# A two-axis Toeplitz block: v stored as pairs of channels, column sums on four 64x64 tiles

## The reference

```python
xn = srms(x)
u = silu(xn @ u_w.T + u_b)
v = silu(xn @ v_w.T + v_b)
out = tno(v, axis=-3, rpe2) + tno(v, axis=-2, rpe1)   # per channel: sum over j of a[i - j] * v[j]
out = (u * out) @ o_w.T + o_b + x
```

## Time and profile before

| | us |
|---|---|
| median of 3 runs (840.05 to 843.59) | 843.44 |
| the profiled execution | 840.65 |
| its span | 838.6 |
| PE busy | 780.2 |
| ScalarE busy | 637.2 |
| VectorE busy | 527.5 |
| GpSimd busy | 282.0 |

### The profile page before, as it was taken

How to read it: one execution, slowest core, us unless ns; L and a number is a source line. 1 busy time by engine, 2 the same in 40 slices (tenths; PEclk the granted TensorE clock), 3 DMA queues, 4 the chain that set the end, 5 groups by cost and what they waited for, 6 DMA issues and landing times.

```text
span 838.6 us, 16989 instructions
## 1 busy us (share of the span) xinstructions
PE 780.2 (93%) x5996; PEld 725.7 (87%) x5996; DVE 527.5 (63%) x917; ACT 637.2 (76%) x794; POOL 282.0 (34%) x191
## 2 busy tenths in 40 slices
PE   0999979999999999899999999989999999897886
PEld 0999879999999999799999999979999999765654
DVE  7666534259999999444554445455655665676666
ACT  0666657789999998777788787769999999665554
POOL 4334332221112112645555454210000001866664
PEclk9999999999999999999999999989999999999999
DMA  9455463497777675688888888685445444777876
GB/s 222 135 158 176 148 164 142 166 222 159 169 167 173 140 162 158 195 279 260 273 268 275 273 262 275 196 199 121 113 120 125 113 116 143 223 250 247 253 249 190
DMA packets 128985, 160.97 MB, mean 192 GB/s; under 512 B 67288, under 2 KB 94108, under 8 KB 128924
## 3 DMA queue, kind: packets, MB, share of 16 engines
q1 hardware_dynamic: 128924, 160.15, 68.2%
HBM read 109.49 MB, written 50.63 MB: 191 GB/s over the span
## 4 chain that ended last, share of the span: by engine, by line
PE 80%; DMA 12%; DVE 2%; ACT 1%; issue 1%; SPq 1%; POOL 1%; POOLq 0%; ACTq 0%; DVEq 0%
PE ps L946 24%; PE ps L1011 16%; PE ps L1024 15%; DMA out<-x_e 9%; PE ps L993 8%; PE ps L966 6%; PE ps L956 5%; PE ps L937 3%; POOL u_in L471 1%; PE ps L969 1%; SPq L269 1%; DMA u_dram<-u_in 1%; DMA stage<-a_dram 1%; DMA u_in<-u_dram 1%; PE ps L920 1%
## 5 line engine op out<-in xcount | busy, mean ns | idle before, releaser
L471 POOL TENSOR_TENSOR u_in<-u_in,v 128x1152 f32<-128x1152 f32 (+2 forms) x66 | 171.4, 2602 | 191.7 <-DMA u_in<-u_dram 175.8
L564 ACT COPY vc<-v 128x1024 f32<-128x1024 f32 x72 | 170.8, 2372 | 6.3 <-DMA out<-x_e 6.3
L848 DVE TENSOR_TENSOR g<-ps,g 128x512 fp32r<-128x512 f32 (+1 forms) x192 | 125.6, 681 | 73.0 <-ACT g L536 45.7
L1011 PE MATMUL ps<-vc,toepA 128*128 128x128 f32 x1152 | 144.1, 279 | 6.1 <-DVE toepA L802 4.2
L1011 PEld LDWEIGHTS ps<-vc,toepA 128*128 128x128 f32 x1152 | 137.3, 195 | 6.7 <-issue 6.4
L1024 PE MATMUL ps<-toepB,vt 128*128 128x128 f32 x1152 | 140.5, 275 | 0.0
L1024 PEld LDWEIGHTS ps<-toepB,vt 128*128 128x128 f32 x1152 | 134.8, 192 | 0.0
L802 DVE COPY toepA<-stage 64x512 f32<-64x512 f32 x144 | 110.0, 764 | 33.5 <-DMA stage<-a_dram 15.2
L742 DVE TENSOR_TENSOR xl<-ps,xh 96x512 fp32r<-96x512 f32 x64 | 44.0, 687 | 130.4 <-ACT xh L512 130.4
L946 PE MATMUL ps<-wu,xh 97*128 97x288 f32 x512 | 122.8, 305 | 2.4
L946 PE MATMUL ps<-wv,xh 97*128 97x288 f32 x512 | 119.3, 308 | 4.6 <-ACT u_in L517 4.2
(11 more groups left out here) (75 smaller groups left out, 1004.9 us busy)
## 6 DMA issues: line engine op xcount, KB each, us to landing
stage<-a_dram SPq DMA_DIRECT2D x144, 256.0 KB, 4.2
u_in<-u_dram SPq DMA_DIRECT2D x64, 576.0 KB, 5.3
u_dram<-u_out SPq DMA_DIRECT2D x48, 576.0 KB, 3.3
x_e<-in_x_eT SPq DMA_DIRECT2D x64, 192.0 KB, 3.8
out<-x_e SPq DMA_DIRECT2D x64, 192.0 KB, 3.8
u_dram<-u_in SPq DMA_DIRECT2D x16, 576.0 KB, 2.9
x_all<-in_x SPq DMA_DIRECT2D x16, 384.0 KB, 5.3
x_n<-in_x SPq DMA_DIRECT2D x16, 384.0 KB, 5.4
```

The source lines that it names most:

```text
L471: return nc.gpsimd.tensor_tensor(out=tile, in0=tile, in1=v[:, bass.ds(t * NB, NB), start:end], op=ALU.mult)
L564: nc.scalar.copy(vc[n % 2][:], v[:, :, UNIT * n:UNIT * n + UNIT].rearrange("p m c -> p c m")).then_inc(vc_ready, 1)
L848: nc.vector.tensor_tensor(out=low, in0=ps[0:w, bank], in1=high.bitcast(f32), op=ALU.subtract).then_inc(gl_ready, 1)
L1011: last = nc.tensor.matmul(ps[:, SET_BANK[n % 2] + c // NB, (c % NB) * P:(c % NB + 1) * P], toepA[n % 2][:, c], vc[n % 2][:, c], start=(c % ...
```

## The change

v is stored as pairs of channels: `v[128, 144 pairs, 128 columns, 2]`, so that one channel of all columns has a step of 8 bytes. The copy `vc` and its semaphore go; PE reads v itself.

`along_columns` now works on four tiles of 64x64. `toepA` is `[128, 8, 64]`, without zero blocks and made by one copy. For each c of 0 to 3, channel c goes through the tiles (rows 0 to 63, outputs 0 to 63) and (64 to 127, 64 to 127), channel 4 + c through the two crossed ones, so that its two rows of pixels land in PSUM exchanged. For those channels the transposes use `swap`, the identity with its halves exchanged, and `evacuate_y` puts them back with two copies of 64 partitions, three copies in all. Each tile's last matmul increments `columns_done`.

The SiLU into v and the gate follow the new order of v. GpSimd no longer zeroes toepA. What lay beside v in the first projections (x, the weights, the network's matrices and activations) now lies in the second halves of v's rows, `free_rows`, which are free until step 16, and has more and smaller pieces in its DMAs; chunks 4 to 7 of x are loaded to three other places, `x_late`, and chunk 7 is loaded at the head of chunk 5, not of chunk 4. Of the diff, what follows leaves out changed offsets, the counts of semaphores and the same rewriting of operands in other lines.

```diff
-        v = place("v", [P, STEPS * NB, D], 0)
-        w_raw = place("w_raw", [KE, 2, D], 0)
-        x_all = place("x_all", [P, STEPS, NB, E], V_BYTES - STEPS * NB * E * 4)
-        R0 = 79104
-        r_lw = place("r_lw", [P, 2, LAYERS, RC, RPE], R0)
...
+        v = place("v", [P, D // 2, STEPS * NB, 2], 0)
+
+
+        free_rows = place("free_rows", [P, D // 2, 2, P], 0)
+
+        def rows(first, count, width=P, partitions=slice(0, P)):
+            return free_rows[partitions, first:first + count, 1, 0:width]
...
+        x_late = [place(f"x_late{k}", [P, CHUNK_ROWS, E], V + offset) for k, offset in enumerate((36864, 13824, 0))]
+
+        def x_chunk(c):
+
+            if c < FREE_CHUNKS:
+                return rows(CHUNK_ROWS * c, CHUNK_ROWS, E)
+            return x_late[(c - FREE_CHUNKS) % 3][:]
...
         stage = [place(f"stage{k}", [P, 2, H, UNIT], V + U_BYTES * k) for k in range(STAGES)]
-        toepA = [place(f"toepA{k}", [P, UNIT, P], V + (50688, 40960)[k]) for k in range(2)]
+        toepA = [place(f"toepA{k}", [P, UNIT, H], V + (50688, 52736)[k]) for k in range(2)]
         toepB = [place(f"toepB{k}", [P, UNIT, P], V + (32768, 28672)[k]) for k in range(2)]
-        vc = [place(f"vc{k}", [P, UNIT, P], V + (13824, 18432)[k]) for k in range(2)]
...
+        Y_PARTS, TILES = 3, 4
+
         def conv_through(engine, half, unit):
 
-            engine.wait_ge(conv_out, UNITS * half + unit + 1)
+            engine.wait_ge(conv_out, Y_PARTS * (UNITS * half + unit + 1))
...
                 for i in range(2):
-                    sp.dma_start(x_all[H * i:H * i + H, CH * c:CH * (c + 1)].rearrange("p s n e -> p (s n) e"),
-                                 rows_of(0, CH * c, CH, i)).then_inc(x_all_loaded, 16)
+                    sp.dma_start(x_chunk(c)[H * i:H * i + H], rows_of(0, CH * c, CH, i)).then_inc(x_all_loaded, 16)
...
+                for o in range(RC):
+                    sp.dma_start(rows(lw_row(n, o, 0, 0), LAYERS * RC),
+                                 lwT[n].rearrange("l (c p) (o q) -> o p (l c) q", p=P, q=P)[o]).then_inc(rpe_loaded, 16)
+                for c in range(RC):
+                    sp.dma_start(rows(OW + NCH * (RC * n + c), NCH, E),
+                                 out_wT[n, P * c:P * c + P].rearrange("p (h q) -> p h q", h=NCH)).then_inc(rpe_loaded, 16)
...
             def phase_a(c, first, last):
-                if c + 3 < CHUNKS:
+                if c + 3 < CHUNKS - 1:
                     load_x_all(c + 3)
+                elif c + 2 == CHUNKS - 1:
+
+                    sp.wait_ge(x_scaled, CH * (c + 2 - 2))
+                    load_x_all(c + 2)
...
             nc.gpsimd.affine_select(out=ident[:], in_=ident[:], compare_op=ALU.not_equal, fill=1.0, base=0,
                                     pattern=[[-1, P]], channel_multiplier=1).then_inc(consts_ready, 1)
 
+            pool.wait_ge(consts_ready, 1)
+            for k in range(2):
+                nc.gpsimd.tensor_copy(swap[:, H * k:H * k + H], ident[:, H - H * k:P - H * k]).then_inc(consts_ready, 1)
...
                     nc.gpsimd.memset(tile[H * k:H * k + H, :, H - H * k:P - H * k], 0.0).then_inc(toep_zeroed, 1)
                     pool.wait_ge(toep_zeroed, count + k + 1)
 
-            pool.wait_ge(a_stored, 32)
-            zero(toepA[0], 0)
-            pool.wait_ge(norms_summed, CHUNKS)
-            pool.wait_ge(x_scaled, STEPS)
-            zero(toepA[1], 2)
             pool.wait_ge(projected, PAIRS * STEPS)
-            zero(toepB[0], 4)
+            zero(toepB[0], 0)
...
             def gate(half, t, r, loads, start=0, end=D):
 
                 pool.wait_ge(u_loaded[r % CH], 16 * CHUNKS * half + 16 * loads)
-                tile = u_in[:, r % CH, :, start:end]
+                tile = u_in[:, r % CH, :, start:end].rearrange("p n (c e) -> p n c e", e=2)
                 return nc.gpsimd.tensor_tensor(
-                    out=tile, in0=tile, in1=v[:, bass.ds(t * NB, NB), start:end], op=ALU.mult)
+                    out=tile, in0=tile, in1=v[:, start // 2:end // 2, bass.ds(t * NB, NB)].rearrange("p c n e -> p n c e"),
+                    op=ALU.mult)
...
-            def silu(xs, pair, target):
+            def silu(xs, pair, target, source):
                 act.wait_ge(projected, PAIRS * xs + (pair + 1))
-                b = 2 * (pair % 2)
-                nc.scalar.activation(target, ps[:, b:b + 2, 0:D], ACT.Silu).then_inc(silu_done, 1)
+                nc.scalar.activation(target, source, ACT.Silu).then_inc(silu_done, 1)
...
+            def projection(pair):
+                return ps[:, 2 * (pair % 2):2 * (pair % 2) + 2, 0:D]
 
             def silu_v(half, t, pair):
                 if half:
                     act.wait_ge(ug_ready, t + 1)
-                silu(STEPS * half + t, pair, v[:, bass.ds(t * NB + 2 * pair, 2)])
+                silu(STEPS * half + t, pair, v[:, :, bass.ds(t * NB + 2 * pair, 2)],
+                     projection(pair).rearrange("p n (c e) -> p c n e", e=2))
...
-            def by_channels(half, n):
...
-                nc.scalar.copy(vc[n % 2][:], v[:, :, UNIT * n:UNIT * n + UNIT].rearrange("p m c -> p c m")
-                     ).then_inc(vc_ready, 1)
...
 
                 def evacuate_y(n):
                     act.wait_ge(conv_done, UNITS * half + n + 1)
-                    bank = SET_BANK[n % 2]
-                    nc.scalar.copy(v[:, :, UNIT * n:UNIT * n + UNIT],
-                                   ps[:, bank:bank + 2].rearrange("p b (c m) -> p m (b c)", m=P)).then_inc(conv_out, 1)
-
-                by_channels(half, 0)
+                    bank, pair, pairs = SET_BANK[n % 2], UNIT // 2 * n, UNIT // 4
+                    nc.scalar.copy(v[:, pair:pair + pairs],
+                                   ps[:, bank].rearrange("p (c e m) -> p c m e", e=2, m=P)).then_inc(conv_out, 1)
+
+                    for i in range(2):
+                        to, of = slice(H * i, H * i + H), slice(H - H * i, P - H * i)
+                        nc.scalar.copy(v[to, pair + pairs:pair + 2 * pairs],
+                                       ps[of, bank + 1].rearrange("p (c e m) -> p c m e", e=2, m=P)
+                                       ).then_inc(conv_out, 1)
+
                 evacuate_vt(0)
                 for n in range(UNITS):
                     if n:
                         evacuate_y(n - 1)
                     if n + 1 < UNITS:
-                        by_channels(half, n + 1)
                         evacuate_vt(n + 1)
...
+                    if axis == 0:
+                        nc.vector.tensor_copy(
+                            toepA[n % 2][:], stage[n % STAGES][:, axis].rearrange("p k c -> p c k")[:, :, ::-1]
+                        ).then_inc(toepA_ready, 1)
+                        return
...
                         nc.vector.tensor_copy(
-                            (toepA, toepB)[axis][n % 2][rows, :, rows],
+                            toepB[n % 2][rows, :, rows],
                             stage[n % STAGES][rows, axis].rearrange("p k c -> p c k")[:, :, ::-1]
-                        ).then_inc((toepA_ready, toepB_ready)[axis], 1)
+                        ).then_inc(toepB_ready, 1)
...
@@ -991,33 +1019,30 @@
                     wait(pe, vt_ready, N)
                     for c in range(UNIT):
                         last = nc.tensor.transpose(ps[:, VT_BANK + c // NB, (c % NB) * P:(c % NB + 1) * P],
-                                                   v[:, :, UNIT * n + c], ident[:])
+                                                   v[:, UNIT // 2 * n + c // 2, :, c % 2], (ident, swap)[c // NB][:])
...
                 def along_columns(n):
+
+                    N = UNITS * half + n
+                    pe.wait_ge(toepA_ready, N + 1)
+                    if n >= 2:
+                        conv_through(pe, half, n - 2)
+                    for c in range(NB):
+                        for i, o, b in ((0, 0, 0), (1, 1, 0), (0, 1, 1), (1, 0, 1)):
+                            of, to, ch = slice(H * i, H * i + H), slice(H * o, H * o + H), NB * b + c
+                            last = nc.tensor.matmul(ps[to, SET_BANK[n % 2] + b, c * P:(c + 1) * P],
+                                                    toepA[n % 2][of, ch], v[of, UNIT // 2 * n + ch // 2, :, ch % 2],
+                                                    start=(c == 0), stop=False, skip_group_check=True)
+                            if c == NB - 1:
+                                last.then_inc(columns_done, 1)
+
+                def along_rows(n):
 
                     N = UNITS * half + n
                     if n < 2:
-                        pe.wait_ge(toep_zeroed, zeroed_for(n)[n][0])
-                    pe.wait_ge(toepA_ready, 2 * (N + 1))
-                    pe.wait_ge(vc_ready, N + 1)
-                    if n >= 2:
-                        conv_through(pe, half, n - 2)
-                    for c in range(UNIT):
```

(19 more changed lines are left out.)

111 lines of the change are left out of this document (52 added, 59 removed).

## The result

| | before | after |
|---|---|---|
| median of the runs | 842.98 us | 814.50 us (813.19 to 815.15, 4 runs) |
| ratio | 1 | 0.967, 95% interval 0.965 to 0.969 |
| span of the profiled execution | 838.6 us | 812.3 us |

The account below looks back on a forecast made before the run. TensorE, busy 93%, was taken to bound the kernel. 840.65 + 28.8 (tile shape) + 1.5 (ScalarE) - 2.4 (VectorE) + 0.3 (loads) + 0.5 (start) = 869.35 us; the median lies 2.8 above, so 872 us, range 800 to 900.

Parts of the forecast that it names:

- What bounds it: Whole kernel: TensorE is busy for 93% of the span, and inside the sums a change pays on PE alone.
- a record costs its 128 columns: Matmul records on PE: 0.112 us for 128 moving columns, whatever part of the array is filled.
- The columns: Column sums on four 64x64 tiles: half the overlap lost to program order, 1.79 us a unit as before, no change.
- Rival 1: Column sums: all four tiles run at once, columns with shape changes 1.29 us, unit 3.97, total 807 us; chance 0.40.
- the forecast: The prediction's main case: half the tile overlap lost to program order, total 872 us; chance 0.42.
- The change of tile shape: Into and out of the column sums: 0.20 us each, 0.40 us a unit, +28.8 us over 72 units.
- The reads of v: Column sums: PE reading one float in two of v as moving operand costs nothing, 0 us.
- ScalarE, silu, gate: Three evacuating copies at 0.59 us each, silu into v at 0.65 us, gate at 2.67 us; new layout costs 0.
- the 4.0 us that was set against it: GpSimd's gate by the skill's rule that reads at steps over 8 bytes are half again as dear: +5 us.
- the +1.5: Ends of the two sums stages: ScalarE's three copies have nothing to hide behind, +0.8 us twice, +1.5 us.
- VectorE and the starts: Starts of both sums stages: no vc copy to await, toepA made in one copy; -1.7 and -0.7, together -2.4 us.
- Loads of x: First projections: store of u earlier, -4 us; chunk 7 loaded later, +4.3 us; net +0.3, bounds -5 and +5.

## Why the prediction was wrong, step by step

**What bounds it, and that a record costs its 128 columns: right**, for tiles too. Each tile keeps 0.112 us (two tiles: 32 records in 1.78 us).

**The columns: wrong, and this is the whole miss.** I took a value between two ends 2.7 us a unit apart, 1.79 us (called the middle, though halfway would be 2.23), by a rule that no row supported: program order without any look-ahead. Measured 0.89 us; the term was 0 and should have been -0.90 x 72 = -65 us. The rule is not empty. It holds from the fifth record in a row on one tile (four matmuls in a row: 2.4 us), but a float32 matmul is two. The Trainium skill does not in fact stand on both sides. The Trainium skill's TensorEngine Tiling (Array Packing), Key Properties, has tiles load and multiply in parallel, and the trace agrees: four records, one for each tile, every 0.11 us. The sentence on strict order in start and end, from the Trainium skill's TensorE: Matmul & The Clock Gate, Part 3, was read out of its place. That part is itself about packing small tiles, and its picture has the matmuls of different tiles start some 4 ns apart and run at once, so it was no ground for 1.79 us. Where the sentence is taken by itself, this case differs: with four in a row a tile's first record starts before the last three of the tile before. Rival 1 named the condition, a queue deep enough for a whole pair, and gave 807 us; with the first projections 5.8 us longer instead of its 0.8 it would be 812, against the 814.5 measured (part of that closeness is chance, since it had nothing for the reads of v and 0.02 to 0.04 us a unit too much for the changes of shape). I gave it 0.40 and the forecast 0.42: the chances were nearly even, and the forecast's number hung on the smaller fact.

**The change of tile shape: right.** 0.18 us was read from the earlier trace rows and rounded to 0.20; measured 0.17 to 0.19 in the kernels with small tiles. Term +28.8, measured about +27. The place in the earlier trace rows was a change to one stationary row, not to a tile of 64x64; that both cost the same was a guess that came out.

**The reads of v: missed, small.** Term 0; measured 0.10 us a unit, +7 us. I asked only about the moving operand (0.03 of it). The larger part, 0.06, is in the transposes, whose stationary v went from a step of 1152 bytes to 8; the run with reads side by side gives back more than both. I took their pace for that of the moving columns, and it is not.

**ScalarE, silu, gate: right.** 0.581 to 0.586 us for 0.59, 0.653 for 0.65, 2.72 for 2.67 (and not the 4.0 us that was set against it). The end of a sums stage is 1.8 us of copies (688.44 to 690.23) instead of 1.0: the +1.5 in two.

**VectorE and the starts: about right.** The sums stages fell by 32.5 us, of which 0.45 x 72 - 1.5 = 30.9 are the units and the ends; 1.6 are left for the starts, where I had 2.4. It came out partly by chance: in the kernel before, the first columns at 172.02 took 3.45 us because the clock was at its lower level (granted 0.51 from 172.3 to 175.8), some 1.7 us that no term held and that the changed kernel does not lose, while its waits for toepA and toepB take some of it back. "What is late next is the stage load" shows:

```profile
189.62 1.06 DVE L826 COPY toepA<-stage 128x512 f32<-128x512 f32 x1 [4.57 <-DMA stage<-a_dram]
```

**Loads of x: mechanism right, size wrong.** ScalarE's old stall shrank from 5.07 to 2.18 us. The kernel with the earlier load, which has neither stall in full, is the measure for both: from step 20 to step 26 it takes 25.2 us, the kernel before 29.2 and the changed one 33.1. The old stall thus cost the 4 us forecast for it, though in part by the clock (granted 0.51 from 117.7 to 121.1). The new one was put at +4.3 us and cost 7.9, because the load took 6.7 us instead of the median 5.3, and because I left out the clock: the wait of 5.6 us of PE is followed by 5.5 us of work at 1.2 GHz, some 2.7 us lost. Net +3.9 for my +0.3, within the bound of +5.

**Not seen at all**: r_diag, +1.5 us, by the loop that became straight code.

The sum with the measured terms (columns, changes of shape, reads, ends, starts, loads, r_diag): -65 + 27 + 7 + 1.5 - 1.6 + 3.9 + 1.5 = -25.7 us, against -26.3 of the spans.

## What to carry to other kernels

If a block-diagonal matmul wastes half of the array in both directions, four 64x64 tiles give the factor of two, but only with all four in use and with one, at most two, float32 matmuls in a row on the same one; count 0.2 us for each change of shape, and put the small-tile work of several units together. When the forecast hangs on one mechanism whose ends are far apart and no row lies between, its number should not be the middle because it is the middle: say that the case is open. And an edit that leaves PE idle in mid-kernel can cost a half-clock stretch besides that time (here after 5.6 us, and once after 1.4), so look at every load that such a change moves in its queue.

## What the runs showed of the hardware that was not expected

- TensorE hands out records in program order, with up to three waiting for a busy tile, and those of another tile start before them: a new tile joins 0.51 us after the last one when each has eight records in a row.
- A change between 128x128 and 64x64 tiles costs 0.18 to 0.19 us, seen on the way back to 128x128 as idle time of the weight loads with no releaser.
- A float32 transpose of 128x128 takes 0.119 us with its stationary operand at a step of 8 bytes, 0.111 at 1152 bytes and 0.102 side by side.
- VectorE's r_diag (128x128, from SBUF to SBUF) takes 0.28 us alone and 0.93 us where a GpSimd operation of 0.83 us starts 0.02 us behind it: it waits out the operation, and does not share with it.
- A wait of PE of 1.4 us was followed by 6.8 us at 1.2 GHz in one kernel and by none in another.
